# A decoder layer with experts: GpSimd's hand-over stretch as one sequence, slot tables as single operations, five queues in another order

## The reference, cut to what matters

```
x = x + attn(layernorm(x))            # 16 batches of 256 tokens, width 256, causal, with a slope
x = x + cross_attn(layernorm(x), ctx) # 16 heads of 16, then @ wfc.T
x = x + ffn(layernorm(x))

def ffn(x):                                       # 8 experts, the top 2 for each token
    probs = softmax(x @ w_gate)
    top_v, top_i = top_k(probs, 2);  gates = top_v / sum(top_v)
    g, u = split(x @ w_gate_up[e]);  act = silu(g) * u      # F = 1024
    return sum over the two experts of gate_e * (act @ w_down[e])
```

## Time and profile before

| | |
|---|---|
| median of 3 runs | 1072.26 us (1071.54 to 1072.60) |
| the profiled execution | 1069.32 us, span 1067.5 us |
| PE busy | 998.5 us, 94% of the span, 12720 matmuls |
| weight loads of PE | 833.8 us |
| DVE / ACT / POOL busy | 641.9 / 628.5 / 537.4 us |
| chain that ended last | PE 75%, DVE 7%, issue 5%, DMA 4%, ACT 4%, POOL 3% |
| mean granted clock of PE | 0.983 |

### The profile page before, as it was taken

The page is one execution under the profiler, slowest core; times in us unless marked ns, Lnnn a source line. Parts: engine busy times, 40 slices in busy tenths (PEclk is TensorE's granted clock), DMA queues, the critical chain, the costliest instruction groups (busy, mean ns, idle before and its releaser), DMA issues.

```text
span 1067.5 us, 36427 instructions
## 1 busy us (share of the span) xinstructions
PE 998.5 (94%) x12720; PEld 833.8 (78%) x12720; DVE 641.9 (60%) x2082; ACT 628.5 (59%) x1343; POOL 537.4 (50%) x582
## 2 busy tenths in 40 slices
PE   5689999999999999967989999999999999999996
PEld 4356666666666666635989999999999999999886
DVE  6677888888888888863566444444444444444333
ACT  6589898888888888855343333333333333333332
POOL 6856777777777777623344332232332323333342
PEclk9799999999999999998999999999999999999999
DMA  6855665667666565359744555962654753335552
GB/s 195 258 181 161 181 184 191 198 198 197 182 178 202 162 190 175 112 120 310 198 69 61 144 92 151 275 176 50 173 162 106 224 159 62 48 51 168 165 153 24
DMA packets 146247, 167.74 MB, mean 157 GB/s; under 512 B 75008, under 2 KB 123200, under 8 KB 141824
## 3 DMA queue, kind: packets, MB, share of 16 engines
q1 hardware_dynamic: 130910, 148.66, 46.3%
q0 software_dynamic: 15248, 18.18, 10.5%
q10 hardware_dynamic: 18, 0.01, 0.0%
HBM read 270.75 MB, written 43.07 MB: 294 GB/s over the span
## 4 chain that ended last, share of the span: by engine, by line
PE 75%; DVE 7%; issue 5%; DMA 4%; ACT 4%; POOL 3%; SPq 1%; DVEq 0%; ACTq 0%; POOLq 0%
PE front L2744 16%; PE t_ring L2744 15%; PE pv L2774 7%; PE s_ring L2774 7%; PE pv L2521 5%; PE s_ring L2488 4%; PE t_ring L2506 3%; PE front L2371 3%; PE front L2362 3%; PE front L2421 2%; PE tail L2371 2%; POOL w_halves L905 1%; DMA xn_t<-xn_h 1%; DVE nmax L1580 1%; DMA rows<-normed,row_i 1%
## 5 line engine op out<-in xcount | busy, mean ns | idle before, releaser
L1004 POOL DMA_INDIRECT out<-y_sb,place_i x64 | 100.5, 1571 | 281.0 <-DVE y_sb L2117 109.1
L2744 PE MATMUL front<-rows_t,wgu_sb 128*128 128x128 f16 x3072 | 195.0, 221 | 2.2 <-DVE act_t L2124 1.6
L2744 PE MATMUL t_ring<-rows_t,wgu_sb 128*128 128x128 f16 x3072 | 192.6, 219 | 0.0
L2744 PEld LDWEIGHTS front<-rows_t,wgu_sb 128*128 128x128 f16 x3072 | 184.9, 99 | 6.0 <-issue 2.2
L2744 PEld LDWEIGHTS t_ring<-rows_t,wgu_sb 128*128 128x128 f16 x3072 | 182.4, 98 | 3.4 <-issue 0.6
L1177 ACT ACTIVATE probs_t<-t_ring,mask_bias 128x512 f32<-128x512 f32 x256 | 164.4, 699 | 15.9 <-PE t_ring L2506 11.7
L1580 DVE TENSOR_REDUCE nmax<-s_ring 128x2 f32<-128x512 f32 x256 | 165.3, 683 | 13.0 <-PE s_ring L2488 10.7
L1338 ACT ACTIVATE silu_g<-t_ring 128x256 f32<-128x256 f32 x136 | 51.8, 383 | 156.2 <-PE t_ring L2744 141.6
L2124 DVE SCALAR_TENSOR_TENSOR act_t<-t_ring,silu_g 128x256 f32<-128x256 f32 x136 | 57.6, 424 | 142.6 <-ACT silu_g L1338 142.2
L1338 ACT ACTIVATE silu_g<-front 128x256 f32<-128x256 f32 x136 | 52.0, 384 | 153.9 <-PE front L2744 141.9
L2124 DVE SCALAR_TENSOR_TENSOR act_t<-front,silu_g 128x256 f32<-128x256 f32 x136 | 57.7, 424 | 127.9 <-ACT silu_g L1338 127.5
(11 more groups left out here) (314 smaller groups left out, 1860.9 us busy)
## 6 DMA issues: line engine op xcount, KB each, us to landing
wgu_sb<-gu_split SPq DMA_DIRECT2D x68, 2048.0 KB
wd_sb<-down_split SPq DMA_DIRECT2D x68, 1024.0 KB
w_piece<-in_w_gu SPq DMA_DIRECT2D x32, 512.0 KB, 6.6
gu_split<-w_halves SPq DMA_DIRECT2D x32, 512.0 KB, 3.8
w_piece<-in_w_down SPq DMA_DIRECT2D x16, 512.0 KB
down_split<-w_halves SPq DMA_DIRECT2D x16, 512.0 KB, 4.4
x_in<-in_x SPq DMA_DIRECT2D x16, 256.0 KB, 2.9
ctx_in<-in_ctx_t_in SPq DMA_DIRECT2D x16, 256.0 KB, 3.2
```

The source lines that it names most:

```text
L1004: nc.gpsimd.indirect_dma_start(out=out, out_offset=bass.IndirectOffsetOnAxis(ap=place_i[:, j:j + 1], axis=0), in_=y_sb[:, j], in_offset=No ...
L2744: o = nc.tensor.matmul(gu_ring[f][:, part * SLOT:(part + 1) * SLOT], wgu_sb[j][:, w, at:at + P], rows_t[:, j, NC * r + c], start=(i == 0), ...
```

## The change

The waits `behind_exps` and `behind_gates`, which held some of GpSimd's scatters and one gather back, are gone. GpSimd's calls from batch 14 to slot 7 stand in one `ending()`, in another order. Each table function has one part for each operation, and a part now waits for the operation before it at its start, so that other work can stand between two of them. The other four queues have their calls in another order. No operation is added to any engine or taken from it. The diff, cut:

```diff
 # SP
             def ending():
                 first_entries()
                 entries_at(2, 2)
+                entries_at(3, 3)
                 entries_at(1, 1)
                 load_first(0)
-                entries_at(3, 3)
+                next_entries(0)
+                entries_at(5, 1)
                 transpose_normed(B - 3, 1)
+                entries_at(7, 3)
                 first_rows(0)
+                load_first(2)
+                first_rows(1)
                 load_first(1)
                 load_first_down(0)
-                load_first(2)
-                next_entries(0)
-                entries_at(5, 1)
+                transpose_normed(B - 2, 0)
+                load_first_down(1)
+                store_normed(B - 3, 1)
+                first_rows(2)
+                first_rows(3)
+                reload_gate_up(0, 0)
+                load_first(3)
+                store_stream(B - 3)
+                load_first_down(3)
+                reload_rows(0, 0, 0)
+                reload_gate_up(1, 1)
+                entries_ahead(0, 0)
+                load_first_down(2)
+                reload_down(1, 1)
+                reload_gate_up(2, 2)
+                store_stream(B - 2)
                 entries_at(6, 2)
-                store_stream(B - 3)
-                first_rows(1)
-                transpose_normed(B - 2, 0)
-                load_first(3)
...
+                reload_rows(1, 1, 0)
+                entries_ahead(1, 1)
+                store_stream(B - 1)
                 reload_down(0, 0)
+                transpose_normed(B - 1, 1)
+                reload_rows(2, 2, 0)
+                reload_rows(3, 3, 0)
...
 # GpSimd: before
-            scatter_first(B - 4, 0, B // 2 - 2)
-            scatter_part(0, 1)
-            out_rest(B - 3)
-            scatter_part(0, 2)
-            scatter_part(0, 3)
-            rsqrt_tail(B - 3)
-            xn3_rest(B - 3, 1)
...
-            gather(0, 0, 0)
-            behind_exps(1)
-            gather(1, 1, 0)
-            out_rest(B - 2)
-            scatter_first(B - 3, 1, B // 2 - 1)
-            behind_exps(4)
-            scatter_part(1, 1)
-            rsqrt_tail(B - 2)
-            behind_exps(6)
-            xn3_rest(B - 2, 0)
...
 # GpSimd: after
+            def ending():
+                scatter_first(B - 4, 0, B // 2 - 2)
+                scatter_part(0, 1)
+                scatter_part(0, 2)
+                scatter_part(0, 3)
+                out_rest(B - 3)
+                rsqrt_tail(B - 3)
+                xn3_rest(B - 3, 1)
+                first_gather()
+                gather(1, 1, 0)
+                scatter_first(B - 3, 1, B // 2 - 1)
+                out_rest(B - 2)
+                scatter_part(1, 1)
+                gather(2, 2, 0)
+                rsqrt_tail(B - 2)
+                scatter_part(1, 2)
+                xn3_rest(B - 2, 0)
+                gather(3, 3, 0)
+                gather(4, 0, 1)
+                scatter_part(1, 3)
+                scatter_first(B - 2, 0, B // 2 - 1)
+                scatter_part(0, 1)
+                scatter_part(0, 2)
+                scatter_part(0, 3)
+                gather(5, 1, 1)
+                out_rest(B - 1)
+                gather(6, 2, 1)
+                rsqrt_tail(B - 1)
+                first_results()
+                gather(7, 3, 1)
+                xn3_rest(B - 1, 1)
+                results(1)
+                results(2)
+                gather(8, 0, 2)
...
 # VectorE: one of the 18, 19 and 29 parts, and the start of its order
+                if part == 1:
+                    vec.wait_ge(slot_step, step[0])
+                    then(nc.vector.tensor_copy(count_i[:], count[:]))
...
-                h_max(B - 1, 0, 2)
-                early_table(2)
-                h_max(B - 1, 2, 4)
+                h_max(B - 1, 0, 2)
+                early_table(12)
...
+                early_table(17)
                 t_add(B - 3)
                 t_stats3(B - 3)
+                h_max(B - 1, 2, 4)
                 t_aggr3(B - 3)
+                slot_rows(0, 0, 0)
+                t_var3(B - 3)
                 h_max(B - 1, 4, 6)
-                t_var3(B - 3)
+                t_norm3(B - 3)
+                slot_rows(1, 1, 0)
+                slot_rows(2, 2, 0)
                 h_max(B - 1, 6, 8)
-                t_norm3(B - 3)
+                slot_rows(3, 3, 0)
                 h_max(B - 1, 8, 10)
...
 # ScalarE
                 h_exp(B - 1, 1, 1)
+                t_ont(B - 2)
                 h_exp(B - 1, 2, 0)
+                h_exp(B - 1, 2, 1)
                 h_out(B - 1, 1, 0)
-                t_ont(B - 2)
-                h_exp(B - 1, 2, 1)
...
 # TensorE
                 t_gate(B - 3)
+                first_gate_up(0, 0, 0)
                 first_scores_t(B - 1, 1)
                 h_scores_t(B - 1, 1, 0, 1)
-                first_gate_up(0, 0, 0)
+                gate_up(0, 0, 1)
                 h_scores_t(B - 1, 1, 1, 0)
+                t_rank(B - 3)
...
                 h_scores_t(B - 1, 1, 7, 1)
+                gate_up(0, 0, 2)
                 h_values(B - 1, 1, 6)
                 h_values(B - 1, 1, 7)
-                gate_up(0, 0, 2)
                 t_gate(B - 2)
                 gate_up(0, 0, 3)
                 first_gate_up(1, 1, 0)
...
                 gate_up(3, 3, 1)
+                t_fc(B - 1)
+                t_fc_rest(B - 1)
                 gate_up(3, 3, 2)
+                down(2, 2, 0, 0)
                 gate_up(3, 3, 3)
...
+                first_gate_up(4, 0, 1)
+                gate_up(4, 0, 1)
                 down(3, 3, 0, 0)
-                gate_up(4, 0, 1)
+                gate_up(4, 0, 2)
+                gate_up(4, 0, 3)
                 t_gate(B - 1)
                 down(3, 3, 0, 1)
```

More of the change, by code:

```diff
@@ L1037, in _, with first_gather @@
-            gather(3, 3, 0)
+            def first_gather():
+                for p in range(2):
+                    pool.wait_ge(normed_out[p], 16 * ((EARLY_TOKENS + 1 - p) // 2 + 1))
+                gather(0, 0, 0)
             def results(s):
                 scatter_results(s, s % STREAMS, s // STREAMS)
[L1042 to L1074, removed]
@@ L1075, in _, with first_results @@
-            results(6)
-            results(7)
+            def first_results():
+                pool.wait_ge(stream_out, 16 * B)
+                pool.wait_ge(pads_out, 32)
+                results(0)
+            def ending():
[32 more added lines that the diff above has]
+                gather(8, 0, 2)
+                results(3)
+                gather(9, 1, 2)
+                scatter_first(B - 1, 1, B // 2)
+                scatter_part(1, 1)
+                results(4)
+                scatter_part(1, 2)
+                scatter_part(1, 3)
+                gather(10, 2, 2)
+                results(5)
+                gather(11, 3, 2)
+                results(6)
+                results(7)
@@ new lines, in early_table @@
+                if part == 2:
+                    vec.wait_ge(slot_step, step[0])
+                    then(nc.vector.tensor_scalar(slots_i[:], count_i[:], SLOT.bit_length() - 1, None,
+                                                 ALU.arith_shift_right))
+                if part == 3:
+                    vec.wait_ge(slot_step, step[0])
+                    then(nc.vector.tensor_copy(slots_f[:], slots_i[:]))
+                if part == 4:
+                    vec.wait_ge(slot_step, step[0])
+                    then(nc.vector.tensor_tensor_scan(slot_end[:], one_e[:], slots_f[:], 0.0, ALU.mult, ALU.add))
@@ new lines, in early_table @@
+                if part == 11:
+                    vec.wait_ge(slot_step, step[0])
+                    then(nc.vector.tensor_reduce(slot_e[:, 0:0 + EARLY], past[:, 0:EARLY], AX.X, ALU.add))
+                if part == 12:
+                    vec.wait_ge(slot_step, step[0])
+                    then(nc.vector.tensor_scalar(slot_ec[:, 0:0 + EARLY], slot_e[:, 0:0 + EARLY], float(E - 1), None, ALU.min))
+                if part == 13:
+                    vec.wait_ge(slot_step, step[0])
+                    then(nc.vector.tensor_copy(slot_tab[:, 1, 0:0 + EARLY], slot_ec[:, 0:0 + EARLY]))
@@ new lines, in early_table @@
+                if part == 14:
+                    vec.wait_ge(slot_step, step[0])
+                    then(nc.vector.tensor_reduce(slot_r[:, 0:0 + EARLY], past_jump[:, 0:EARLY], AX.X, ALU.add))
+                if part == 15:
+                    vec.wait_ge(slot_step, step[0])
+                    then(nc.vector.scalar_tensor_tensor(slot_r1[:, 0:0 + EARLY], slot_order[:, 0:0 + EARLY], float(SLOT), slot_r[:, 0:0 + EARLY],
+                                                        ALU.mult, ALU.add))
@@ new lines, in late_table @@
+                if part == 14:
+                    vec.wait_ge(slot_step, step[0])
+                    then(nc.vector.tensor_reduce(slot_r[:, EARLY:EARLY + LATE], past_jump[:, 0:LATE], AX.X, ALU.add))
```

(6 more changed lines are left out.)

554 lines of the change are left out of this document (323 added, 231 removed).

## The result

| | kernel before | changed kernel |
|---|---|---|
| median of 6 runs | 1072.38 us | 1079.55 us |
| lowest to highest | 1071.21 to 1072.60 | 1078.35 to 1082.75 |
| profiled execution, its span | 1069.3, 1067.5 | 1078.62, 1076.9 |

The ratio is 1.0074 (95% interval 1.0058 to 1.0089): the change makes the kernel 7.2 us slower. 1067.0 had been forecast, with a range up to 1074.5, so the forecast has the wrong sign.

What follows compares the result with a forecast made beforehand. TensorE, busy 94%, was taken as the bound, with only its waits and lowered clock from about 450 to 543 us winnable: 0.7 + 1.8 + 2.4 + 0.4 = 5.3 us, 1072.3 to 1067.0 us, range 1060.5 to 1074.5.

Steps and rivals of the forecast that it cites:

- The tables as single operations, slots 4 to 7, and the rest: Single table operations and slots 4 to 7: VectorE covers them and PE has no idle time there, 0 us.
- a new idle stretch of PE in slots 4 to 8: Sign named as one that would show the forecast wrong, at slots 4 to 8; no size given.
- A: Up to the end of batch 15's attention: earlier scatters, loads and slot 0's rows, gain 0.7 us (-2.0 to +3.0).
- B: Wait at batch 14's gate product: its transpose goes out sooner behind drained loads, gain 1.8 us (0 to 4.2).
- C: Clock after batch 14's gate product: stays at 1.00, 48 matmuls cost 2.84 us, gain 2.4 us (0 to 2.4).
- D: Batch 15's gate product: PE waits 3.0 us instead of 3.48, gain 0.4 us (-3.0 to +4.8).
- the condition that the prediction had attached to a negative D: SP held at reload_rows(0, 0, 0) or (1, 1, 0), so that the store goes out 3 us later.
- Ahead of the stretch: Before about 450 us: no gain or loss priced; only about 450 to 543 us was said to change the time.
- The longer wait for batch 15: Rival at batch 15's gate product: store 3 us late, one more microsecond of clock, 1071.0 us, chance 0.14.
- Late rows: Rival at slot 0: rows land late, PE stands before first_gate_up(0, 0, 0), attention shifts, 1076.8 us, chance 0.17.
- All waits gone: Rival at the gate products: all waits for xn_t go, 12.4 us gained, 1059.9 us, chance 0.13.
- The rule of the Trainium skill: Against A: gather(1, 1, 0)'s 1.4 us add to batch 13's transpose and slot 0's rows, making the sum 3.9 us.

Runs made afterwards that it cites:

- r_gu4: Changed kernel with plain DMA copies for its DMA transposes, and reload_gate_up(4, 0) moved on SP ahead of reload_rows(4, 0, 1): 1070.01 us.
- r_both: r_gu4 with GpSimd's xn3_rest(B - 1, 1) also moved ahead of first_results() and gather(7, 3, 1): 1067.56 us.
- h_after: Changed kernel with each DMA transpose replaced by a plain DMA copy of the same bytes: 1074.75 us.
- t_after: Same kernel as h_after (changed kernel with plain copies for its DMA transposes), run in another group: 1078.18 us.
- r_before: Kernel before with plain DMA copies in place of its DMA transposes, on one chip with r_after: 1070.53 us.
- r_after: Same kernel as h_after (changed kernel with plain copies for its DMA transposes), on one chip with r_before and r_gu4: 1075.82 us.
- s_both: Same kernel as r_both, run in another group: 1078.75 us, ratio 1.0000 to the kernel before.

## Why the prediction was wrong

**The step that failed is the one priced at nothing: "The tables as single operations, slots 4 to 7, and the rest: 0 (-0.5 to +0.3)".** It gave a reason for the tables (VectorE has room) and none for SP's calls of slots 4 to 7, which the diff moves as freely as the others. One of them, `reload_gate_up(4, 0)`, went from ahead of `reload_rows(3, 3, 0)` to behind `reload_down(5, 1)`. Slot 8 lost 4.3 us in the wait, 0.2 just ahead of it and 1.6 in the clock behind it (0.91 over 20 us). The wait is in the trace of the changed kernel itself. That it, and not another behind it, is the loss is shown with plain copies, by r_gu4: with the one call moved, 5.8 us come back. The same step stands at the head of the prediction, which kept to 450 to 543 us "apart from what it leaves late for later slots" and looked at no later slot, and at its end, which named "a new idle stretch of PE in slots 4 to 8" as what would make it wrong, without pricing it.

**The other terms**, measured as changes of the lag:

- *A, 0.7 us.* It lost 1.0. TensorE is done with batch 15's attention at 503.34, where the idle time before 504.29 begins, and in the kernel before at 498.27: the lag grows from 4.1 to 5.1. The first weight load, at 470.64, is 2.0 us behind the forecast's 464.5 and the lag, so no sooner than before. Slot 0 begins 0.9 us behind its 478.0 and the lag. `gate_up(0, 0, 1)` was priced at 1.34 us, but ran at 486.35 with a granted clock of about 0.6, in 2.49. Batch 15's exponentials start at 486.28, 1.1 us behind 481.1 and the lag.
- *B, 1.8 us.* It came, 1.7: the wait at batch 14's gate product fell from 2.66 to 0.95 us, although the transpose goes out at 500.33, 2.2 us behind 494.0 and the lag. Together the two gave 0.7 us of 2.5 (lag 4.1 to 3.4), and the term that was mis-sized is A.
- *C, 2.4 us.* It came: the 48 matmuls at 507.71 take 2.84 us, clock 1.00, after an idle stretch of 1.61.
- *D, 0.4 us.* From there to slot 7 the lag grows from 1.0 (3.4 less C's 2.4) to 3.7, a loss of 2.7. GpSimd's chain is the one forecast (result scatter, gather, subtraction), but SP issues the `x_res` store at 535.57 and not at 524.2 plus the lag: `t_add` was done at 530.06, and then SP was held at the rows of slot 5 (532.83) and an entry, the condition that the prediction had attached to a negative D. r_both shows what the subtraction's place costs: 3.5 us of wait at the gate product, of which 1.6 reach slot 5. The wait of 1.8 us for `act_lo` at 532.48, behind an entry's load, was not foreseen.
- *Ahead of the stretch, 0 us.* 4.1 in the profiled pair. 1.8 of it is there at the first gate product (106.12 against 104.36), for which both transposes took 3.2 us. Most of the rest comes near 386 and 415 us, where two of the changed kernel's transposes of `xn_t` take 4.3 and 4.5 us to land (one near 131 takes 4.0); all thirteen of the kernel before in the batch loop take 3.1 to 3.2. But the fifteen runs with plain copies, whose batch loop is one and the same code, reach the last gate product of the loop anywhere from 443.7 to 446.8 us (442.81 and 446.95 in the real pair); h_after and t_after, one kernel, are 1.6 apart there, r_before and r_after 1.7. So a lag of most of this size comes without any transpose and without a change. Slot 8 less the 0.4 us gained ahead of it is 5.7 of the 7.2 us between the medians; that leaves 1.5, and the interval of the difference runs from 6.2 to 9.5 us. Whether the rest is a part of this lag stays open.

The sum closes: -1.0 + 1.7 + 2.4 - 2.7 - 6.1 = -5.7, with -4.1 ahead -9.8, against 9.4 between the spans.

**The rivals.** The longer wait for batch 15 happened, 4.21 us for 3.48, but gave only part of its 4. Late rows did not: slot 0 began at 482.96, less the lag 478.9, where 478.0 was forecast. All waits gone is false. The rule of the Trainium skill (DMA: Bandwidth & Descriptors, Issuing engines are not separate DMA queues), that transfers of all issuing engines interleave on the same engines, had batch 13's product 1.4 us later than 476.2; it came at 481.52, less the lag 477.4. That is 1.2 us late, but it doesn't bear the rule out: the transpose went out at 475.36, less the lag 471.3, where 470 was forecast, and then took 6.1 us, where 6.2 was assumed. The lateness is that of the issue, and no run here shows the 1.4 us of the gather's bytes.

## What to carry to other kernels

In a queue that is issued in order, price every call that changed its place, whatever it does: ask what it signals, who waits for that and when, and what now stands ahead of it. A load that is skipped still carries a signal, and here the place of one was worth 6 us. And follow a changed order to the last consumer of the last moved call, two or three slots behind the last line of the diff.

## What the runs showed of the hardware

- A skipped load, with its register reads, takes SP about 1.5 us. Two of them and an entry, between a late transpose and the load that mattered, put it 5.6 us behind the end of the transpose's issue (574.29 to 579.92), though the two moved nothing.
- With plain copies the kernel before is 0.4 to 0.7% faster (0.9933, 0.9958, 0.9943 in three groups). A copy of `xn_t` lands after 2.4 us, the transpose after 3.1 to 3.2. How much of the gain is that isn't shown, since the routing differs too.
- In three of the five groups TensorE had short gaps, 0.3 to 1.2 us, many of them some 0.75 us apart, in most kernels near 525 and 565 us, with no releaser in the trace. The Trainium skill (Runtime: NRT & Kernel Launch, Instruction fetch mechanics) says that an engine's instructions are fetched in blocks ahead of their use and that this is mostly hidden; no run here shows whether these gaps are that fetch.
- The kernel before differs by 0.4% between the groups, and one variant by 1.0% (r_both, s_both), so they order variants differently: r_both beats r_before, s_both loses to s_before. A gain of under 1% that one group shows clear of its interval can be missing in the next. No version that beats both kernels in each group was found.
